# Tensor-product layer of a graph network: weights formed from stored transposed units, tiles taken in pairs

## What is computed

```python
def _forward(x, edge_src, edge_dst, edge_vec, emb, norm, W1, W2):
    xs = jnp.concatenate([x[edge_src, :8], x[edge_dst, :8]], axis=1)
    xv = jnp.concatenate([x[edge_src, 8:].reshape(E, 8, 3), x[edge_dst, 8:].reshape(E, 8, 3)], axis=1)
    y1, y2 = _sph(edge_vec)
    h = 2.0 ** 0.5 * jax.nn.relu(emb @ W1 / 10.0 ** 0.5)
    w = (h @ W2 / 16.0 ** 0.5).reshape(E, 7, MUL, MOUT)
    wa_s, wb_s, wa_g, wb_g, wc, wd, we = [w[:, i] for i in range(7)]
    s_out = PW_S * (jnp.einsum('eu,euw->ew', xs, wa_s) + INV_SQRT3 * jnp.einsum('eui,ei,euw->ew', xv, y1, wb_s))
    g_out = ...
    v_out = PW_V * (INV_SQRT3 * jnp.einsum('eu,ek,euw->ewk', xs, y1, wc) + INV_SQRT3 * jnp.einsum('eui,euw->ewi', xv, wd) + jnp.einsum('eui,ea,iak,euw->ewk', xv, y2, W3J121, we))
    s_act = TANH_GAIN * jnp.tanh(s_out)
    gates = TANH_GAIN * jnp.tanh(g_out)
    edge_ftr = jnp.concatenate([s_act, (gates[:, :, None] * v_out).reshape(E, 24)], axis=1) * norm[:, None]
    return jax.ops.segment_sum(edge_ftr, edge_dst, num_segments=N)
```

## Time and profile before

| | us |
|---|---|
| timed runs, median | 16,380.43 |
| profiled execution, span | 13,418.0 |
| PE busy | 6021.0 (45%) |
| DVE busy | 5448.5 (41%) |
| ACT busy | 2111.0 (16%) |
| POOL busy | 7502.6 (56%) |

### The profile page before, as it was taken

How to read it: one execution, slowest core, us unless ns; L and a number is a source line. 1 busy time by engine, 2 the same in 40 slices (tenths; PEclk the granted TensorE clock), 3 DMA queues, 4 the chain that set the end, 5 groups by cost and what they waited for, 6 DMA issues and landing times. The chain is left out here.

```text
span 13418.0 us, 195196 instructions
## 1 busy us (share of the span) xinstructions
PE 6021.0 (45%) x81668; PEld 5074.6 (38%) x81668; DVE 5448.5 (41%) x7142; ACT 2111.0 (16%) x2759; POOL 7502.6 (56%) x7346
## 2 busy tenths in 40 slices
PE   1000000300000599999980000000399999999779
PEld 0000000300000599888970000000266666666578
DVE  4454555900000201111112233323488888888711
ACT  1111111000000000000001122111244444444300
POOL 5777776777777413030207777776655555555150
PEclk6555555555555799999985555555699999999889
DMA  4445453000000599889952111111111111111179
GB/s 173 165 168 189 163 175 122 0 0 0 0 0 0 208 368 358 327 310 343 363 209 42 39 42 42 39 39 23 25 32 32 32 32 32 32 32 33 36 271 340
DMA packets 516083, 1622.37 MB, mean 121 GB/s; under 512 B 233432, under 2 KB 315536, under 8 KB 424144
## 3 DMA queue, kind: packets, MB, share of 16 engines
q1 hardware_dynamic: 258272, 1346.21, 27.0%
q0 software_dynamic: 234368, 154.18, 6.1%
q10 hardware_dynamic: 22640, 110.04, 2.1%
HBM read 1262.48 MB, written 352.41 MB: 120 GB/s over the span
## 5 line engine op out<-in xcount | busy, mean ns | idle before, releaser
L197 POOL DMA_INDIRECT z_l<-table,idx_l x1568 | 1752.6, 1118 | 1234.2 <-DMA dir_p<-unit 739.5
L197 POOL DMA_INDIRECT g_l<-table_l,idx_l x1568 | 1649.2, 1052 | 511.0 <-issue 500.9
L843 POOL DMA_INDIRECT adj<-worth,sq x1568 | 1546.1, 986 | 545.7 <-issue 509.5
L1935 PE MATMUL p_r<-prod_k,ident 128*128 128x256 f32 x6272 | 1705.7, 396 | 239.4 <-DVE prod_k L2199 207.7
L197 POOL DMA_INDIRECT g_gat<-table,idx_gat x1568 | 1479.4, 944 | 514.0 <-issue 499.6
L1935 PEld LDWEIGHTS p_r<-prod_k,ident 128*128 128x128 f32 x6272 | 1132.9, 194 | 425.4 <-DVE prod_k L2199 274.7
L2199 DVE TENSOR_TENSOR prod_k<-p_t,h_l 128x512 f32<-128x512 f32 x1568 | 1071.1, 683 | 0.0
L999 PE MATMUL p_h<-wd,emb_s 80*128 80x128 f32 x392 | 104.2, 444 | 2009.1 <-ACT hid L1053 1847.5
L1567 PE MATMUL pr<-diag,ones 128*128 128x256 f32 x2 | 1.2, 714 | 2110.4 <-DVE diag L1585 2110.4
L407 PE MATMUL pc_l<-spread,cross_lo 128*128 128x448 f32 x28 | 25.3, 1023 | 1853.8 <-DVE spread L411 1690.4
L999 PEld LDWEIGHTS p_h<-wd,emb_s 80*128 80x128 f32 x392 | 87.8, 327 | 2025.4 <-ACT hid L1053 1855.8
(11 more groups left out here) (489 smaller groups left out, 13729.9 us busy)
## 6 DMA issues: line engine op xcount, KB each, us to landing
cells_cheb<-adj SPq DMA_DIRECT2D x560, 1344.0 KB
adj<-zeros SPq DMA_DIRECT2D x28, 7056.0 KB, 26.0
cells_l<-adj SPq DMA_DIRECT2D x140, 1344.0 KB
cells_cheb<-adj SPq DMA_DIRECT2D x56, 672.0 KB
gat_rows<-prod_gat ACTq DMA_DIRECT2D x28, 952.0 KB, 3.8
g_l<-table_l,idx_l POOLq DMA_INDIRECT x1568
start_rows<-zeros SPq DMA_DIRECT2D x28, 896.0 KB, 4.2
scanned_rows<-msg_l ACTq DMA_DIRECT2D x28, 896.0 KB, 9.7
```

Of the source, the lines that this page charges most:

```text
L197: return pool.indirect_dma_start(out=dest, out_offset=None, in_=table_ap, in_offset=bass.IndirectOffsetOnAxis(ap=index, axis=0))
L843: pool.indirect_dma_start(out=adj, out_offset=bass.IndirectOffsetOnAxis(ap=cell[:, t:t + 1], axis=0), in_=worth_u[:, t:t + 1], in_offset=N ...
L1935: last = nc.tensor.matmul(p_r[:].rearrange("p a k w -> p (a k w)"), ident[:], prod_k[q % 2][:, :, :, k:k + 2, :].rearrange("p g t k w -> p ...
```

## The change

The stage between layer 0's messages and the dense passes gains work, layer 2 is written anew.

- In `l0_pass`, while POOL scatters, SP loads W1 repeated in 8 column blocks and W2 (40 DMAs), DVE prepares `w_terms` (f16, 384 columns), `w_vec` (bf16, 128 columns) and the scale `w_unit`; and 224 pieces of 896 edges are made of `hidden_t` [P, T*P], bf16, in DRAM (51 MB): the hidden units with the edges as columns, each unit eight times over the partitions, in parts of bf16. For a piece PE makes two fp32 matmuls of 448 columns, ACT a ReLU and two 32-partition copies, DVE the rest (PSUM minus SBUF) and a 32-partition difference of two SBUF tiles; SP loads and stores, two buffers.
- The norm stage writes `table` from `x_cur`, without DVE's reordering copies.
- In layer 2 the block of weight preparation is gone. A tile takes one matmul of 384 columns (f16, turned inputs by `w_terms`) and one of 128 (`hidden_t` by `w_vec`, the vector weights of each edge); DVE multiplies the first by the hidden units and the second by the vectors, in two operations of 768 elements a pair of tiles. PSUM holds three pairs. `sums` is 16 fp32 matmuls of 160 columns for four tiles, its result one eviction; products run a group ahead of the sums. `reduced` takes 512 elements at steps of 48, `leave` is one operation, `odd_add` is gone. SP loads the indices of chunk c+2 once ACT's `take` has copied the rows of chunk c out, and `hidden_t` in two halves a chunk.

```diff
@@ l0_pass, weights and transposed units @@
+                        for k in range(8):
+                            sp.dma_start(w1r[:, 16 * k:16 * k + 16], w1).then_inc(w1r_in, 16)
...
+                        def load_emb(k, b):
+                            sp.dma_start(emb_q[b], emb_t[:, bass.ds(k * HB, HB)]).then_inc(emb_in[b], 16)
+
+                        def store_parts(k, b):
+                            sp.wait_ge(ht_third, k + 1)
+                            sp.dma_start(hidden_t[:, bass.ds(k * HB, HB)], parts_q[b]).then_inc(ht_out[b], 16)
...
+                        with v.Fori(0, n_ht) as i:
+                            for b in range(2):
+                                k = 2 * i + b
+                                v.wait_ge(ht_first, k + 1)
+                                V.scalar_tensor_tensor(rest_h[b], pre_h[b], 0.0, parts_h[b], ALU.max, ALU.subtract).then_inc(ht_rest, 1)
+                                v.wait_ge(ht_second, k + 1)
+                                V.tensor_tensor(parts_q[b][96:P, :], rest_q[b][96:P, :], parts_q[b][96:P, :], ALU.subtract).then_inc(ht_third, 1)
...
+                                for h in range(2):
+                                    last = nc.tensor.matmul(pre_h[b][:, h, :], w1r, emb_q[b][:, h * HALF_B:(h + 1) * HALF_B],
+                                                            start=True, stop=True)
...
+                                act.wait_ge(ht_made, k + 1)
+                                act.wait_ge(ht_out[b], 16 * (i + 1))
+                                A_.activation(parts_h[b], pre_h[b], ACT.Relu).then_inc(ht_first, 1)
+                                act.wait_ge(ht_rest, k + 3)
+                                A_.activation(parts_q[b][32:64, :], rest_q[b][32:64, :], ACT.Copy)
+                                A_.activation(parts_q[b][96:P, :], rest_q[b][96:P, :], ACT.Copy).then_inc(ht_second, 1)
@@ norm stage @@
-                            V.tensor_copy(sq[:, js, 0:M], x_cur[:, js, 0:M])
-                            V.tensor_copy(sq[:, js, M:D].rearrange("p j (i m) -> p j m i", i=3),
-                                          x_cur[:, js, M:D].rearrange("p j (m i) -> p j m i", i=3)).then_inc(s_vdone, 1)
+                            v.sem_inc(s_vdone, 1)
@@ l2_pass, SP @@
                         def next_index(c, b):
-                            sp.wait_ge(z_split, c - 1)
+                            sp.wait_ge(z_taken, c - 1)
                             load_index(c, b)
+                        def next_hidden(c, k):
+                            sp.wait_ge(t_made, c * PRS - PRS + (k + 1) * HT // 2)
+                            load_hidden(c, k)
...
+                        def phase(c, b, index=True, start=True):
+                            other = 1 - b
+                            if index:
+                                next_index(c + 3, other)
+                                next_direction(c + 3, other)
+                            next_hidden(c + 1, 0)
+                            next_rest(c + 1, other)
+                            if start:
+                                next_starts(c + 2)
+                            next_hidden(c + 1, 1)
@@ l2_pass, PE @@
-                            nc.tensor.matmul(into[:, 0, KM:4 * KM], lhs_s, ws[0], start=True, stop=False)
-                            nc.tensor.matmul(into[:, 0, KM:4 * KM], lhs_s, ws[1], start=False, stop=True)
-                            nc.tensor.matmul(into[:, 1, 0:3 * KM], lhs_v, wv[0], start=True, stop=False)
-                            nc.tensor.matmul(into[:, 1, 2 * KM:3 * KM], lhs_s, wx[:], start=False, stop=False)
-                            nc.tensor.matmul(into[:, 1, 0:3 * KM], lhs_v, wv[1], start=False, stop=True).then_inc(t_made, 1)
+                                nc.tensor.matmul(scalar_part(k, t), zt[q % 2][:, tile * P:(tile + 1) * P], w_terms[:], start=True, stop=True)
+                                last = nc.tensor.matmul(vector_part(k, t), h_of[:, place * P:(place + 1) * P], w_vec[:], start=True, stop=True)
...
-                            for k in range(4 * part, 4 * part + 4, 2):
-                                last = nc.tensor.matmul(p_r[:].rearrange("p a k w -> p (a k w)"), ident[:],
-                                                        prod_k[q % 2][:, :, :, k:k + 2, :].rearrange("p g t k w -> p (g t) (k w)"),
-                                                        start=(k == 0), stop=(k == 14))
+                            for k in range(4 * part, 4 * part + 4):
+                                last = nc.tensor.matmul(p_sum_out, ident[:], prod[prod_buffer(b, q)][:, :, k, M:COLS],
+                                                        start=(k == 0), stop=(k == 15))
...
+                                next_products(0)
+                                if q + 2 < Q:
+                                    transposes(b, q + 2)
+                                elif more:
+                                    transposes(other, q + 2 - Q)
+                                last_sums(0)
+                                last_sums(1)
+                                next_products(1)
+                                last_sums(2)
+                                last_sums(3)
@@ l2_pass, DVE @@
-                            V.tensor_tensor(prod_k[q % 2][:, :, t], all_banks[:, 3 * KM:7 * KM], h_k, ALU.mult).then_inc(t_used, 1)
+                            V.tensor_tensor(into[:, :, :, 0:24], scalar_pair(k).rearrange("p t (k f) -> p t k f", k=16), h_b, ALU.mult)
+                            V.tensor_tensor(into.rearrange("p t u (i w) -> p (t u) i w", w=M)[:, :, 3:6, :], w_uw, x_ui, ALU.mult).then_inc(t_used, 1)
...
-                            last = V.tensor_reduce(out6[b][:, 0:2, :, 4 * q:4 * q + 4].rearrange("p g w t -> p g t w"),
-                                                   prod[q % 2][:], AX.X, ALU.add)
+                            last = V.tensor_reduce(out6[b][:, 0, :, 4 * q:4 * q + 4].rearrange("p w t -> p t w"),
+                                                   prod[prod_buffer(b, q)][:, :, :, 0:M].rearrange("p t k w -> p t w k"), AX.X, ALU.add)
...
+                            V.tensor_tensor(zsf[:], zsf[:], zs[b][:, :, 0:32], ALU.subtract).then_inc(d_done, 1)
@@ l2_pass, ACT @@
+                        def take(c, b, times, first=False):
+                            act.wait_ge(gathered[b], 16 * CH * (times + 1))
+                            if not first:
+                                act.wait_ge(t_used, (c - 1) * PRS)
+                            A.activation(zsf[:, :, 0:M], z[b][:, :, 0:M], ACT.Copy)
+                            A.activation(xv[b][:, :, 0:24], z[b][:, :, M:D], ACT.Copy).then_inc(z_taken, 1)
```

700 lines of the change are left out of this document (361 added, 339 removed).

## The result

The kernel after takes 16,287.8 us (median of four runs, 16,268.0 to 16,296.1) beside 16,378.7 before: a ratio of 0.9941, 95% interval 0.9927 to 0.9956. The forecast was 15,733, its range 15,540 to 15,990. The sign was right; of the 647 us forecast, 91 came.

The account below looks back on a forecast made before the run. In layer 2's loop PE and DVE, with equal work, were taken to wait for each other. Terms -663 - 29 - 3 + 45 + 3 = -647 us gave 15,733 us, range 15,540 to 15,990.

Parts of the forecast that it names:

- I make the sum against its span and take the rest as unchanged: Whole kernel: savings reckoned on the 13,418.0 us profile; the 2,962 us up to the timed 16,380.4 held constant.
- Hidden by the scatters, with 320 us to spare: Layer 0: making 224 pieces of transposed units, 1370 us, fits a window of some 1690 us beside POOL's scatters.
- the units outlast the scatters: Rival, layer 0: above 7.5 us a piece the rest is exposed; at 8.5, +224, giving 15,957 us; chance 0.05.
- -663 forecast: Layer 2's loop: 86 us a chunk in place of 109.7, over 28 chunks, -663 us.
- the 0.59 that I took between 0.59 and 1.13: Layer 2's loop: a DVE reduction of 512 elements at steps of 48 takes 0.59 us, as without slowing.
- the forecast's own table of groups: Layer 2's loop, by four tiles: PE steady 5.68 us; DVE 4.05 in light groups, 5.55 to 8.6 in groups 2-9.
- its handoffs of 4 us: Layer 2's loop: waits between engines, 0.28 us a group of four tiles, 4 us a chunk, beyond the 82.1.
- both rivals built on it: PE's sums: weight load paces records, 16,276 us, chance 0.05; or load adds to each record, 17,945 us, chance 0.04.
- The 11 us a chunk that the forecast worked out from it: PE's sums: if the skill's load spacing held, 25 ns on 448 records add 11 us a chunk, about 16,050 us.
- +45 of 0 to 80: Layer 0: the units' last DVE operation slows POOL's scatters by 0 to 80 us; +45 taken.
- The eight loads: Layer 0: eight small loads ahead of the first indices, 0.36 us each, +3 us.
- POOL's floor of 81 us: Layer 2's loop: 56 gathers keep POOL 81 us a chunk; rival that only this floor binds, 15,607 us, chance 0.16.

Follow-up runs that it names:

- e0_before: The kernel before, unchanged, profiled again: span 16,422.8 us, time 16,424.5 us.
- T: Condition of the first timed runs, cause unknown: before takes 16,371 to 16,426 us, and engines crawl in some stages where POOL issues indirect DMAs back to back.
- F: Fast condition, cause unknown, also that of the profile the forecast used (span 13,418.0 us): before takes 13,401 us, after 12,919.1 us.
- e10: The kernel after with 4 of the 224 pieces of transposed units, every chunk reading the same columns: 15,058.8 us, where after takes 16,304.6 in the same job.
- e12: The kernel after, unchanged, once more in T: 16,680.1 us, ratio 1.0163 to before.
- e17_after: The kernel after, unchanged, profiled in F: 12,919.1 us beside 13,401.6 for before.
- e15: The kernel after with layer 2's rows gathered once ahead of its loop, chunks 2 to 27 left out, in F: loop 2550 us, 91.1 a chunk.
- e1: The kernel after with two one-byte POOL memsets behind each gather of layer 2, in T: 16,781.6 us.
- e3: The kernel after with two one-byte POOL memsets behind each of layer 0's 1568 scatters, plus a wait each 56 scatters, in T: 15,291.5 us.
- e11: Two memsets behind each indirect DMA of the dense passes, added to e3 with layer 2's gathers gated by DVE's progress: 14,479.7 us, beside 14,472.1 without.
- e13: Five memsets behind each indirect DMA of the dense passes, added to e3 with layer 2's gathers gated by DVE's progress: 14,513.0 us, beside 14,472.1 without.

## Why the prediction was wrong

**The basis.** "I make the sum against its span and take the rest as unchanged" failed first. The unseen 2,962 us were a fifth of the time, and e0_before shows them in full, in the stages beside indirect DMAs: counting 2365 us for 381, the first four dense passes from 4872 to 7850 where the earlier trace rows's profile has 4517 to 6919, the loop 4829 for 3115. The two numbers stood side by side before any sum was made: a span 18% short of the time is not the profile of that time.

That the sign came out right in T is luck: the change gives 1359 us in one place and takes 1261 in another, and the forecast had neither.

**The units.** "Hidden by the scatters, with 320 us to spare" is the term that ate the gain. The piece was right: 6.1 forecast, 5.9 in F (1324/224) and 5.6 in T behind the scatters (1261/224). In F they end at 4047 and the scatters at 4438, 391 us to spare. In T their cover had gone when they began. The text itself gave the price, "without cover, 1370 us"; 1246 were measured (e10). The rival "the units outlast the scatters" had the place and the sign, but reasoned from the piece's length, where it was the start that slipped: I costed what the new stage takes, not how far the stages queued ahead of it on PE and DVE depend on being quick.

**The loop.** -663 forecast, -517 in F, -1359 in T (-1009 by e12). In F 86 us a chunk became 91.4, and the first chunk's wait shrank from 44.0 to 38.2. DVE's timeline (e17_after) has the reductions start to start:

```profile
10916.76 1.01 DVE L2315 TENSOR_REDUCE agg<-prod 128x32 f32<-128x512 f32 x1
10917.69 0.94 DVE L2307 TENSOR_TENSOR prod<-p_t,h_l 128x768 f32<-128x768 f32 x1
...
10922.62 1.00 DVE L2315 TENSOR_REDUCE agg<-prod 128x32 f32<-128x512 f32 x1
10923.55 1.37 DVE L2285 TENSOR_TENSOR zsf<-spread 128x896 f32<-128x896 f32 x1
```

0.93 us and not the 0.59 that I took between 0.59 and 1.13: 14 x 0.34 = 4.8 us of DVE work a chunk. Not all of it lengthens the chunk. By the forecast's own table of groups the light ones have room (4.39 for PE's 5.68), and in the others DVE falls behind by 11.4 us for 8.7, so 2.7 more reach PE.

The rest is a term that the forecast didn't have. Chunks don't take equal times: in e17, from one chunk's first product to the next one's, 88.5 and some 96 us follow each other, with and without gathers (e15). 88.5 is about the forecast's 86 and the 2.7, so that its handoffs of 4 us fit there. The longer chunk is the one in which PE's hardware loop, two chunks a round, turns. PE's timeline at a turn (e17_after), and the stretch behind it with the granted clock at 0.66, between the 1.2 and the 2.4 GHz level:

```profile
10243.20 0.34 PE L2042 MATMUL p_t<-w_terms,spread 128*128 128x384 f16 x1 [1.70 <-issue]
...
10246.49 3.79 PE L2053 MATMUL p_t<-prod,ident 128*128 128x160 f32 x16 [2.33 <-DVE prod L2310]
```
```profile
10246.00:10251.00 5.00, 4.51 (x21) 4.07 (x22) 0.68 (x1) 0.00 (x0) 3.78 (x5) 0.66 0.12 17
```

PE starts nothing for 1.70 us, then waits 2.33 for a product, and the 16 records behind that last 3.79 us for 2.39 elsewhere; DVE in turn waits 4.40. No run takes the turn out, so that these 7.5 us a round are its price by the timeline alone.

In T the gain is another: before got 6 to 8 of its 56 tiles done during a burst of some 71 us, after some 34 in 80 (17 pairs, e.g. in the burst from 12,305). DVE's extras lie under that burst; whether they are the reason is not shown, and in e12, with the same work under them, bursts let 9 to 18 pairs through.

**PE's sums.** Right. Sixteen records of 160 columns (e17_after):

```profile
10994.12 0.33 PE L2042 MATMUL p_t<-w_terms,spread 128*128 128x384 f16 x1
10994.28 0.22 PE L2043 MATMUL p_t<-w_vec,h_t 128*128 128x128 bf16 x1
10994.33 2.39 PE L2053 MATMUL p_t<-prod,ident 128*128 128x160 f32 x16
10996.57 0.33 PE L2042 MATMUL p_t<-w_terms,spread 128*128 128x384 f16 x1
```

2.24/16 = 0.14 us against 0.136 forecast: the weight load of 0.194 stays hidden, and both rivals built on it fall. A tile's two products take 0.22 as costed, and one of 128 columns with a load of its own is followed after 0.05. The Trainium skill (TensorE: Matmul & The Clock Gate, Back-to-back issue gap) has some 81 ns for such a pair of load and matmul of 128 columns. The rows differ from it. The 11 us a chunk that the forecast worked out from it, an estimate, were 25 ns on each of the 448 records of the sums; at 0.14 us apart they aren't there.

**The small terms.** The scatters in F take 2124 us for 2055, +69, where +45 of 0 to 80 was said; in T nothing, since the units come behind them. From the last attention gather to the first product 427 us became 392 in F, -35 for -32. The eight loads: the scatters begin 2 us later, for +3, which is within what two runs of one kernel differ by (2314 in e17, 2310 in e15). POOL's floor of 81 us: its bursts in F last 79 and 80, and its pause shrinks from 29 us a chunk to some 10, so it isn't the 90% busy of the forecast (1315 of 2000 us) and binds nothing. With the measured terms the sum in F is -517 + 69 - 35 + 2 = -481. The other 20 of the 501 us of span are 15 in the dense and attention stages and 4 in the tail, which the change doesn't touch.

The Trainium skill (SBUF — State Buffer, Who interferes with whom) was cited for what a DVE instruction costs POOL. In T the rows show another side, which the citation doesn't cover: in the burst from 12,305, PE starves where DVE is free.

## What to carry to other kernels

When the profile's span and the timed runs differ by more than a few microseconds, profile again before costing anything. Ask of a stage that is to hide under another not only how long it is but when it can start, and what the queue ahead of it waits for. And where engines crawl beside a long run of indirect DMAs on POOL, count their instructions rather than their elements. Try to gate the DMAs by the consumer's progress: it gave 454 us in T, where memsets between the gathers gave next to nothing. Look in the timeline whether an edit that is meant to space instructions does so, before it is read as a test.

## What the runs showed of the hardware that was not expected

- In T, beside scatters 1.29 to 1.40 us apart, PE started one instruction each 1.40 us (a matmul with its load each 0.08 in F); DVE waited up to 46.6 us in the loop (before, from 11,600 to 15,000) and ACT up to 41.8.
- With DVE busy throughout, gathers of the burst from 12,305 in after (T) last some 1.2 us on average for 0.94.
- At the turn of PE's loop (e17) PE started nothing for 1.70 us, and over the 5 us from 10,246, just behind, the granted clock was 0.66; every second chunk took 7.5 us longer.
- A DVE reduction of 512 elements read at steps of 48 takes 0.93 us start to start (e17); for 1024 in order the forecast had 1.13, worked out from the earlier trace rows.
- Two one-byte POOL memsets between indirect DMAs leave their distance at 1.25 us (e1), 1.29 (e3) and 1.30 (e11); five take 0.23 us and lengthen it from 1.30 to 1.38 (e13).
